# The Wo product of the preceding group in front of the scores in an attention kernel on one core

## The reference

```python
def _attn(xq, xc, Wq, Wk, Wv, Wo, bo):            # layer 0: HEADS = 16, D_HEAD = 64
    q = (xq @ Wq).reshape(B, N, HEADS, D_HEAD)
    k = (xc @ Wk).reshape(B, S, HEADS, D_HEAD)
    v = (xc @ Wv).reshape(B, S, HEADS, D_HEAD)
    scores = jnp.einsum('bnhd,bshd->bhns', q, k) * scale
    attn = jax.nn.softmax(scores, axis=-1)
    out = jnp.einsum('bhns,bshd->bnhd', attn, v).reshape(B, N, HEADS * D_HEAD)
    return out @ Wo + bo
...
x = _attn(_ln(x, g1, b1), _ln(x, g1, b1), Wq1, Wk1, Wv1, Wo1, bo1) + x    # SELF
x = _attn(_ln(x, g2, b2), context, Wq2, Wk2, Wv2, Wo2, bo2) + x           # CROSS
x = _geglu_ff(_ln(x, g3, b3), Wp, bp, Wf, bf) + x                         # GEGLU
# layer 1: small-head cross-attention (CROSS2), then a feed-forward layer (FFN)
```

## Time and profile before

| | before |
|---|---|
| median of three runs | 502.99 us |
| the profiled execution | 502.37 us |
| its span | 500.6 us |
| PE busy | 461.1 us, 92% |
| PE weight loads busy | 418.1 us, 84% |
| DVE busy | 370.6 us, 74% |
| ACT busy | 278.2 us, 56% |
| GpSimd busy | 194.4 us, 39% |
| mean granted PE clock | 0.969 |

### The profile page before, as it was taken

How to read it: one execution, slowest core, us unless ns; L and a number is a source line. 1 busy time by engine, 2 the same in 40 slices (tenths; PEclk the granted TensorE clock), 3 DMA queues, 4 the chain that set the end, 5 groups by cost and what they waited for, 6 DMA issues and landing times.

```text
span 500.6 us, 17564 instructions
## 1 busy us (share of the span) xinstructions
PE 461.1 (92%) x7600; PEld 418.1 (84%) x7600; DVE 370.6 (74%) x652; ACT 278.2 (56%) x505; POOL 194.4 (39%) x218
## 2 busy tenths in 40 slices
PE   5889999999999999999999999979997898949997
PEld 4778889899899898898989889869996776737897
DVE  4679788788788788887888878876866577675572
ACT  4455555654645745657456565464454666635673
POOL 4634552442454354434523344233423222121473
PEclk9989999999999999999999999989999999985899
DMA  7750000000000000000000000000000000000011
GB/s 236 179 157 5 1 3 3 3 3 3 3 2 12 1 11 10 1 12 9 3 10 1 12 9 3 3 1 3 0 8 9 17 10 9 1 0 3 0 39 47
DMA packets 17300, 10.57 MB, mean 21 GB/s; under 512 B 7888, under 2 KB 16272, under 8 KB 17232
## 3 DMA queue, kind: packets, MB, share of 16 engines
q1 hardware_dynamic: 16800, 9.48, 7.0%
q10 hardware_dynamic: 432, 0.07, 0.1%
HBM read 8.50 MB, written 1.05 MB: 19 GB/s over the span
## 4 chain that ended last, share of the span: by engine, by line
PE 79%; DVE 14%; ACT 3%; issue 2%; DMA 1%; POOL 0%; ACTq 0%; DVEq 0%
PE stage L565 11%; PE stage L566 10%; PE stage L567 10%; PE out0p L744 9%; PE scp L697 6%; PE scp L853 6%; PE scp L655 4%; PE out0p L758 4%; PE stage L727 4%; PE scp L727 3%; DVE pr L1122 3%; PE stage L708 3%; DVE mx L1117 3%; DVE veps L1070 2%; PE scp L671 2%
## 5 line engine op out<-in xcount | busy, mean ns | idle before, releaser
L930 ACT ACTIVATE pr<-pr 128x1024 f32<-128x1024 f32 x48 | 50.6, 1055 | 67.1 <-DVE pr L1122 65.8
L1366 POOL TENSOR_TENSOR pr<-pr,rc 128x1024 f32<-128x1024 f32 x32 | 60.3, 1904 | 69.3 <-DVE rc L1152 69.3
L744 PE MATMUL out0p<-wo_of,ot 128*128 128x128 f32 x512 | 65.8, 281 | 0.6 <-issue 0.6
L744 PEld LDWEIGHTS out0p<-wo_of,ot 128*128 128x128 f32 x512 | 59.6, 191 | 3.0 <-issue 0.9
L874 ACT ACTIVATE vt<-stage 64x512 f32<-64x512 f32 x64 | 37.9, 592 | 29.6 <-PE stage L567 28.1
L874 ACT ACTIVATE q_of_heads<-stage 128x512 f32<-128x512 f32 x64 | 34.7, 596 | 21.1 <-PE stage L567 21.0
L1157 DVE COPY vt<-stage 64x512 f32<-64x512 f32 x64 | 44.4, 694 | 2.6 <-PE stage L567 0.6
L1283 POOL TENSOR_TENSOR rstd<-veps,neghalf 128x2 f32<-128x2 f32 x32 | 22.8, 712 | 54.8 <-DVE veps L1070 53.6
L655 PE MATMUL scp<-k_of_heads,q_of_heads 64*64 64x64 f32 x2048 | 38.1, 220 | 4.5 <-issue 3.5
L1096 DVE COPY k_of_heads<-stage 128x512 f32<-128x512 f32 x32 | 22.1, 692 | 26.9 <-PE stage L567 26.9
L1117 DVE TENSOR_REDUCE mx<-scp 128x16 f32<-128x1024 f32 x32 | 39.0, 1217 | 2.9 <-PE scp L655 2.9
(11 more groups left out here) (233 smaller groups left out, 1331.2 us busy)
## 6 DMA issues: line engine op xcount, KB each, us to landing
ctx_in<-in_ctx_dram SPq DMA_DIRECT2D x16, 96.0 KB, 2.0
wo_of<-in_L_xattn_Wo_dram SPq DMA_DIRECT2D x2, 512.0 KB, 9.6
out_dram<-rows SPq DMA_DIRECT2D x8, 128.0 KB, 1.8
rows<-in_x_dram SPq DMA_DIRECT2D x1, 768.0 KB, 9.7
pr<-in_L_xattn_Wq_dram SPq DMA_DIRECT2D x1, 512.0 KB, 4.8
pr<-in_L_xattn_Wk_dram SPq DMA_DIRECT2D x1, 512.0 KB, 6.4
pt<-in_L_xattn_Wv_dram SPq DMA_DIRECT2D x1, 512.0 KB, 7.8
rows<-in_L_xattn_Wq_dram SPq DMA_DIRECT2D x1, 512.0 KB, 8.4
```

The costliest lines, as they stand in the source:

```text
L744: last = nc.tensor.matmul(out0p[:, t * D:(t + 1) * D], ot[:, a // 2, a % 2, t, :], wo_w[s.phase][:, a, :], start=(a == 0), stop=(a == PAIR ...
L930: nc.scalar.activation(pr[t][:, :], pr[t][:, :], ACT.Exp, scale=scale[s.phase]).then_inc(exped, 1)
L1366: nc.gpsimd.tensor_tensor(halves(pr[t][:, :]), halves(pr[t][:, :]), rc[:, t, :, None].to_broadcast([ROWS, H, N]), ALU.mult).then_inc(probs, 1)
```

## The change

In every group of SELF and CROSS but the very first, PE makes the Wo product of each tile of the group before in front of the scores of the same tile, not behind them. Nothing else is changed: the other engines' programs stay word for word, and PE has the same instructions.

```diff
                     if s.is_group(CROSS, 0):
                         pe.wait_ge(loaded_ffn, 16 * 8)
+                    if before:
+                        out_step(before, 0)
                     scores_step(s, 0)
                     if before:
-                        out_step(before, 0)
+                        out_step(before, 1)
                     scores_step(s, 1)
-                    if before:
-                        out_step(before, 1)
                     if last:
```

## The result

The changed kernel takes 516.25 us (median of four runs, 515.62 to 517.8) against 502.53 us for the kernel before on the same chip: ratio 1.0284, 95% interval 1.0247 to 1.0321. Measured once more, beside two of the experiments, the ratio was 1.0272 (1.0218 to 1.0326). The prediction was 516.2 us, with 513.9 us for the span of the profiled execution; that span is 513.9 us.

The account below looks back on a forecast made before the run. It put 79% of the chain of waits on PE, with ACT's queue before the fifth projection deciding the change. Terms 14.2 - 4.1 + 1.1 + 2.1 = 13.3 us gave 516.2 us, 8-in-10 range 511.5 to 521.

Parts of the forecast that it names:

- The place: Fifth projection on PE: waits for an ACT copy queued behind exponential 1, so later scores delay it.
- Ordinary groups: SELF 3 to 7, CROSS 0 and 3 to 6: fifth projection 1.42 us later in each, 14.2 us over ten.
- Holes: PE's waits for issue in scores, where AV1 and scores 0 stand in a row: gone, 4.1 us won back.
- The four groups behind GpSimd's weight steps: SELF 1 and 2, CROSS 1 and 2: 0.37 us late in three, 0 in CROSS 1, in sum 1.1 us.
- Rival A: Scores on PE: the issue holes stay or move into the new order; +17.4, 520.3 us; chance 0.14.
- Rival B: CROSS 7 and CROSS 1: longer PE waits bring one or two more lower-clock stretches, 518 to 519.6 us; chance 0.10.
- C: Ordinary groups: delay partly absorbed, exponential 1 only 0.7 us late instead of 1.42; 509 us; chance 0.09.
- D: Fifth projection: its copy not held by exponential 1, only mended holes remain, not slower; 498.9 us; chance 0.04.
- E: Whole PE program: its order does not matter since the work is the same; 503 us; chance 0.03.
- The last group: CROSS 7, no projections: second value product waits for DVE's gated half, all 2.07 us reach PE.
- Sum: Whole kernel: 14.2 - 4.1 + 1.1 + 2.1 = 13.3 us longer.
- The waits: PE before the fifth projection 1.2 to 1.4 us, some 1.7 in CROSS 1; DVE for scores about 22 us in all.

Follow-up runs that it names:

- the second experiment: Kernel before with only tile 1's Wo product moved in front of its scores (PE order scores 0, Wo 0, Wo 1, scores 1): 518.3 us, ratio 1.0326.
- the third experiment: Changed kernel with ACT's copies of the first four projections, not the first alone, in front of exponential 1: 510.11 us, ratio 1.0156 to the kernel before.
- tile 0 alone: Kernel before with only tile 0's Wo product moved in front of its scores (Wo 0, scores 0, scores 1, Wo 1): 507.65 us, ratio 1.0108.
- last group alone: Changed kernel with only the last group of CROSS back in the old PE order: 511.55 us, ratio 1.0235 to the kernel before.
- both scores first: Kernel before with PE order scores 0, scores 1, Wo 0, Wo 1: 505.49 us, ratio 1.0128.

## Why the prediction was right

**The place.** The fifth projection, behind exponential 1 and one copy on ACT, is where the groups with projections lose, all but CROSS 1. Shown by taking it away: with the copies in front, the wait of 18.9 us is gone except for 1.5 us in SELF 0, which has no group before it, and with DVE's copy moved too the groups are within 0.34 us of the kernel before (19.39 against 19.05), which is the mode change.

**Ordinary groups.** Predicted 1.42 each and 11.42 from AV1 to the fifth projection; measured 1.49 and 11.49 (11.58 in SELF 7). Of the 0.07, 0.04 is the start of scores 1 (6.15, not 6.11) and 0.02 DVE's start behind their end (84.57 + 1.16 = 85.73, start 85.80). So ten groups would be 14.9, not 14.2.

**Holes.** Predicted gone, worth 4.1 us. They are gone. The ten groups together lengthened by 9.8 us (the sum of the differences of that distance), so the holes gave 14.9 - 9.8 = 5.1. Those on scores gave 4.0 of it, close to the forecast; the term was too small since it counted only these: one in AV1 of SELF 6 and one in the Wo product of CROSS 6 went as well, 1.0 together. Rival A did not happen. It would have if AV1 and the first scores still stood in a row: that is the second experiment. Rival B did not happen either: the only lower clock in SELF and CROSS behind SELF 0 follows the last group's wait, as before. C, D and E are excluded by the 1.49 in the groups without a hole.

**The four groups behind GpSimd's weight steps.** Predicted 1.1 us; measured 0.43, 0.43, 0.00 (CROSS 1) and 0.66, together 1.5. In CROSS 2 I had taken SELF 2's figure, but GpSimd's step is shorter there (1.27 us, not 2.35) and maximum 0 starts 4.34 behind AV1, in SELF 2 4.57, so less of the delay was hidden. The 0 of CROSS 1 was right for another reason than I gave. It is not the mended hole: in both kernels maximum 0, behind DVE's statistics and GpSimd's step, starts only 5.44 after AV1 and maximum 1 at 7.82, later than the scores are there in either order.

**The last group.** Predicted 2.07; measured 13.40 - 11.27 = 2.13, and the trace of the kernel with the old order in that group has it back at 2.0 us of wait.

**Sum.** 9.8 + 1.5 + 2.1 = 13.4, less 0.35 because AV1 of SELF 1 started that much earlier in this execution (37.34 against 37.69), is 13.1 where 13.3 was forecast. Ordinary groups were forecast 0.7 too low, holes 1.0 too low with the other sign, the weight-step groups 0.4 too low: the exact match of the span is in part luck. So is that of the time, which also needs the changed kernel's median to lie as far above its profiled execution (0.63) as the kernel before's (0.62).

**The waits.** PE's wait was predicted at 1.2 to 1.4 and is 1.1. That was a slip in working out: my own distances have the first projection 1.09 behind scores 1 and the fifth 3.08 behind that, so PE is ready at 84.02 + 1.09 + 3.08 = 88.19 and waits 1.14 until 89.33. In CROSS 1 the wait is 1.41 where I had 1.7. PE does start its projections 0.5 earlier there, as forecast, which from 1.06 gives 1.6 and not 1.7; the rest went in a hold-up of some 0.15 us among the first four projections. DVE's waits were predicted at 22 us and are 21.4. That nothing behind the fifth projection had to be paid for is right; the third experiment shows that the next such place was DVE's copy of the sixth projection, 0.6 us late once ACT's is cured.

## What to carry to other kernels

When work is reordered on an engine that is busy all the time, its own sum does not change; follow the result that has become later to the queues of the engines that use it, and look at what stands behind it there. Such a loss can be cured at that queue, by letting the copies on which the busy engine waits overtake the late instruction: with these five changed lines the same PE order went from 2.8% slower to 1.0% faster. And where rows of very short instructions show holes that nothing else explains, long instructions between them can take the holes away, as the Wo product did here.

## What the runs showed of the hardware

- Rows of 64 tiny matmul records (17 ns each) in succession outrun the instruction stream: holes on scores are 12.2 us in all with three rows (AV1 and both scores), 3.5 to 4.3 with two (AV1 and scores 0), 0.3 to 0.9 with the two score rows alone behind a Wo product, none in the changed kernel, where 2 us of Wo product stand in front of the scores of each tile. The longest was 1.58 us. Every one of 42 holes ended 2.2 to 2.8 us after a block of 16 KB had started on the instruction queue. The Trainium skill, "Runtime: NRT & Kernel Launch", section "Instruction fetch mechanics", calls the crossing of a block mostly hidden; for such rows these runs disagree.
- A change between 64 x 64 and 128 x 128 matmuls and back costs PE 0.35 us (groups of SELF at 19.39 and 19.04 us that differ in nothing else).
- CROSS 1's PE wait of 1.41 us was followed by the lower clock in two profiled executions (tile 0 alone, last group alone) and not in three others (the changed kernel twice, both scores first); where it fell, the group took 1.5 us longer. The last group's wait of 2.0 us was followed by it in two executions and not in four, at a price of 1.6 us.
